# A linear attention block with a gated feed-forward layer: one call moved in the vector engine's program

## The chip, the cores and the metric

The kernel runs on one core of a Trainium2 chip. The core's engines are TensorE (PE; its weight loads are listed apart, as PEld), VectorE (DVE), ScalarE (ACT), GpSimd (POOL) and SyncE (SP), which here only issues DMAs. The metric is the device time of one execution in microseconds (us), the median of three runs. An engine takes its own instructions strictly in the order in which they are written, and the engines meet at semaphores.

## The reference

Sixteen batches of 512 tokens with 256 channels pass through one block of linear attention and one gated feed-forward layer, with a layer norm after each:

```python
qkv = relu(x @ qkv_weight.T)                      # 32 heads of 8 channels: q, k, v
vk   = einsum('bnhe,bnhd->bhed', [v, 1], k)       # per batch and head, 9 x 8
vk_q = einsum('bhed,bnhd->bnhe', vk, q)           # 8 numerators and 1 denominator
att  = vk_q[..., :8] / (vk_q[..., 8:] + 1e-15)
x1   = layernorm(x + att @ proj_weight.T + proj_bias)
h    = silu(x1 @ wg.T) * (x1 @ wu.T)              # wg, wu, wd: integers / 127; hidden 768
out  = layernorm(x1 + h @ wd.T)
```

All of it is float32. The kernel gets that precision from TensorE by splitting each operand into a high part (rounded to fp32r) and a low part (the value minus the high part), so each product is two or three matmuls.

## The kernel before

The 16 batches go through a software pipeline. Step i, for i from 2 to 14, does the feed-forward layer of batch i-1 up to its hidden layer (`ffn_half`), then projection, first layer norm and the turning of batch i, the q, k, v of batch i+1, the down projection of batch i-1, and the attention of batch i+1 (`attention_half`). Steps 2 and 14 are written out, steps 3 to 13 are a hardware loop; the first batches and the last have code of their own. Every engine has its own order, written out by hand; nothing is scheduled by a program.

One step on TensorE is, in order: six gate and up blocks (`gate_up`, j = 0 to 5, eight 128x512 matmuls each), the projection (24 small matmuls), k and v (24), q (12), `vk` (64 tiny ones, L946), the first quarter of the down projection, `num` (64 tiny matmuls, L963, which make numerators and denominators of batch i+1 in the four banks of `abcd_ps`), and three more quarters of the down projection. Then the next step begins with gate block 0, which reads `x1T_hi` and `x1T_lo`.

What the names around the change are:

- `x1T` is the first layer norm's output with channels on the partitions. VectorE transposes it in blocks of 32 (`x1_blocks`, into `wu_raw`), two DMAs out to DRAM and two back in (`wd_raw`, named for the weights that it held before) turn the rest. ScalarE rounds it to `x1T_hi` (L346), VectorE subtracts that (`x1T_lo_spread`, L515): two instructions of 128x512, each with two inputs in SBUF, the engines' common memory.
- `rden_of` waits for `num` (semaphore `num_mm`), then adds the epsilon to the denominators, PSUM to SBUF (`den`, L545, semaphore `den_ok`), and takes the reciprocal (`rden`, L549).
- `att_of` multiplies the numerators in PSUM by `rden` (L567, four instructions). `r2_add` adds the down projection and `x1` (L639, twice). `att_blocks` transposes `att` in blocks (L720, twice).
- GpSimd adds the bias to the next input, `xb` (L296): both inputs in SBUF, 128x1024. It starts when `den_ok` says that `den` of this step is made. GpSimd also makes the inverse deviations, `rstd` (L280).
- `h_of` (L522) makes one of the six blocks of `h` from `up_ps` and `silu`, `h_lo_of` (L515) makes its low part from two inputs in SBUF. `stats_2` (L591) stands between h block 0 and h block 1.

On TensorE the weight load for x1T of gate block 0 waits for both `x1T_lo`; that of gate block 1 waits for the first `r2_add`, since the block overwrites a down bank. From block 2 on, the gate part waits for `silu` of block j-2 and the up part for `h` of block j-2, which free the PSUM banks of that block. ScalarE's order in a step is silu 0, h_hi 0, silu 1, h_hi 1, silu 2, h_hi 2, silu 3, the two `attT_hi`, h_hi 3, silu 4, silu 5, h_hi 4 and 5; a silu stands behind the h_hi before it.

Of the kernel before, what the change touches and what calls it, by code (L numbers as in the profile page):

```python
# [38 lines left out]
def build(nc, x, xT, q_w, kv_w, proj_w, bias, gate_w, up_w, down_w, shape_consts, out):  # L39
    ctx = ExitStack()  # L40
    with ctx:
# [467 lines left out]
        def _(dve):  # L509
# [4 lines left out]
            def minus_hi(lo, raw, hi):  # L514
                return nc.vector.tensor_tensor(lo, raw, f32(hi), ALU.subtract)  # L515
# [10 lines left out]
            def h_lo_of(b, *blocks):  # L526
                for j in blocks:
                    dve.wait_ge(h_hi_ok[j], b + 1)
                    minus_hi(h_lo[:, j, :], h[:, j, :], h_hi[:, j, :]).then_inc(h_lo_ok[j], 1)

            def xT_lo_of(b):
                dve.wait_ge(xT_hi_ok, b)
                minus_hi(xT_lo[:], xT_raw[:], xT_hi[:]).then_inc(xT_lo_ok, 1)

            def vk_of(b, bank=CC):

                dve.wait_ge(vk_mm, b + 1)
                vkv = bank[:, 0:KC * VW].rearrange("p (k n) -> p k n", k=KC)
                nc.vector.tensor_tensor(vk[:], vkv.unsqueeze(2).to_broadcast([P, KC, 2, NW]),
                                        own[:].unsqueeze(1).to_broadcast([P, KC, 2, NW]), ALU.mult).then_inc(vk_ok, 1)  # L540

            def rden_of(b):

                dve.wait_ge(num_mm, b + 1)
                nc.vector.tensor_scalar(  # L545
                    den[:].rearrange("p m (t g u) -> p m (t g) u", t=NT, g=2),
                    num_ps[:, :, :, :, GC:NW].rearrange("p m t g u -> p m (t g) u"), DEN_EPS, None, ALU.add).then_inc(den_ok, 1)
                dve.wait_ge(den_ok, b + 1)
                nc.vector.reciprocal(rden[:], den[:]).then_inc(rden_ok, 1)  # L549

            def att_of(b, turned=False):

                dve.wait_ge(rden_ok, b + 1)
                if turned:

                    for t in range(NT):
                        for m in range(2 * KC):
                            last = nc.vector.tensor_tensor(
                                att[:, t, m // 2 * P:(m // 2 + 1) * P].rearrange("p (u e j) -> p j u e", j=NG, e=HD)
                                [:, m % 2 * 2:m % 2 * 2 + 2],  # L560
                                num_ps[:, m, t, :, 0:GC].rearrange("p j (u e) -> p j u e", e=HD),
                                rden[:, m, t * 2 * GH:(t + 1) * 2 * GH].rearrange("p (j u) -> p j u", j=2)
                                .unsqueeze(3).to_broadcast([P, 2, GH, HD]), ALU.mult)
                    last.then_inc(att_ok, 1)
                    return
                for t in range(NT):
                    last = nc.vector.tensor_tensor(  # L567
                        att[:, t, :].rearrange("p (m g u e) -> p m g u e", g=2, u=GH, e=HD),
                        num_ps[:, :, t, :, 0:GC].rearrange("p m g (u e) -> p m g u e", e=HD),
                        rden[:, :, t * 2 * GH:(t + 1) * 2 * GH].rearrange("p m (g u) -> p m g u", u=GH)  # L570
                        .unsqueeze(4).to_broadcast([P, 2 * KC, 2, GH, HD]),
                        ALU.mult)
                last.then_inc(att_ok, 1)
# [38 lines left out]
            def r1_of(b):  # L612

                if not isinstance(b, int) or b > 1:
                    dve.wait_ge(x1_copied, 16 * (b - 1))
                else:
                    dve.wait_ge(x1_pair[1], 1)
                dve.wait_ge(xb_ok, b + 1)
                for n in range(2):
                    r1_pair(b, n)  # L620
                    stats(st1, r1, n, st1_ok if n else None)
# [14 lines left out]
            def r2_add(b, n, x1_of_b):  # L636

                dve.wait_ge(down_mm[n], b + 1)
                nc.vector.scalar_tensor_tensor(  # L639
                    out=pair(r2, n), in0=down_ps[n], scalar=WSCALE, in1=pair(x1_of_b, n), op0=ALU.mult, op1=ALU.add).then_inc(r2_ok[n], 1)  # L640
# [23 lines left out]
            def x1_of(b, dst):  # L664
                dve.wait_ge(rstd1_ok, b)
                normed(dst, r1, mv1, rstd1, x1_ok)

            def out_of(b):

                if not isinstance(b, int) or b > 0:  # L670
                    dve.wait_ge(stored, 16 * b)
                dve.wait_ge(rstd2_ok, b + 1)
                normed(out_sb, r2, mv2, rstd2, out_ok)
# [49 lines left out]
            def x1_blocks(b):  # L723
                dve.wait_ge(x1_ok, b)
                blocks_turned(x1_sq, r1, x1_sq_ok)

            def att_blocks(b):
                dve.wait_ge(att_ok, b + 1)
                blocks_turned(att_sq, att, att_sq_ok)

            def T_lo_spread(b, T_raw, T_hi, T_hi_ok, T_lo, T_lo_ok):
                for k in range(KC):
                    dve.wait_ge(T_hi_ok[k], b + 1)
                    minus_hi(by_token(T_lo, k), spread(T_raw, k), by_token(T_hi, k)).then_inc(T_lo_ok[k], 1)
# [4 lines left out]
            def x1T_lo_spread(b):  # L739
                T_lo_spread(b, x1T_raw, x1T_hi, x1T_hi_ok, x1T_lo, x1T_lo_ok)  # L740
# [24 lines left out]
            def variance_1(i):  # L765
                dve.wait_ge(st1_ok, i)
                nc.vector.tensor_copy(st1_seen[:], st1[:, NT - 1, 0:1])
                aggregated(st1, mv1, mv1_ok)
                variance(i - 1, mv1, mv1_ok, ve1, ve1_ok)
# [29 lines left out]
            def attention_half(i):  # L799
                r1_of(i)  # L800
                variance_1(i)
                h_lo_of(i - 1, 4)
                x1_of(i, r1)
                x1_blocks(i)
                h_lo_of(i - 1, 5)
                out_of(i - 2)
                vk_of(i + 1)
                if not isinstance(i, int) or i + 2 < NB:
                    xT_lo_of(i + 2)
                x1T_lo_spread(i)  # L810
                rden_of(i + 1)
                att_of(i + 1)
                for n in range(2):
                    r2_add(i - 1, n, x1)
                att_blocks(i + 1)
# [3 lines left out]
            first_turn()  # L819
            ffn_half(2)  # L820
            attention_half(2)

            with dve.Fori(3, NB - 2) as i:
                ffn_half(i)
                attention_half(i)

            ffn_half(NB - 2)
            attention_half(NB - 2)

            i = NB - 1  # L830
# [40 lines left out]
            i = NB  # L871
# [339 lines left out]
```

## Time and profile before

| | |
|---|---|
| runs | 501.08, 502.88, 500.78 us |
| median | 501.08 us |
| profiled execution, its own time | 501.08 us |
| its span | 498.9 us |
| TensorE busy | 490.4 us (98%), mean granted clock 0.997 |
| VectorE busy | 421.8 us (85%) |
| ScalarE busy | 228.7 us (46%) |
| GpSimd busy | 87.8 us (18%) |

The span goes from the first instruction's start to the last one's end; 2.2 us of the run's time lie outside it. TensorE's matmuls are pipelined, so their busy shares overlap, and "98%" says only that there is hardly a moment without one. A line of a timeline gives the start, the length, the engine, the source line, the operation, its output and inputs with shapes, and in brackets the idle time before it with what ended it. Where several instructions of one group follow each other they are merged into one line with their count.

### The profile page before, as it was taken

The numbers are of one execution on the slowest core, as the hardware profiler recorded it, in microseconds if no ns is written. First come the engines' busy times: TensorE is split into PE (matmuls) and PEld (weight loads), VectorE is DVE, ScalarE is ACT, GpSimd is POOL, SyncE is SP. The second block draws the span as 40 slices with busy tenths as digits, with TensorE's granted clock in tenths as the row PEclk, the third lists the DMA queues.
The fourth block names the chain that finished last, engine by engine and source line by source line (L and its number), as shares of the span: only waits on it lengthen the run. The fifth ranks groups of instructions, "written<-read, shape, count | busy, mean of one in ns | idle before, by whom it ended". The sixth has DMA issues, their size and how long they took to land.

```text
span 498.9 us, 11667 instructions
## 1 busy us (share of the span) xinstructions
PE 490.4 (98%) x4588; PEld 422.3 (85%) x4588; DVE 421.8 (85%) x986; ACT 228.7 (46%) x384; POOL 87.8 (18%) x69
## 2 busy tenths in 40 slices
PE   8999999999999999999999999999999999999995
PEld 5788888988888888888988888888888988888785
DVE  5778998788989888798888989889798888978996
ACT  4665354353643535444353543535444353533343
POOL 1220211112113111121121113111131122113102
PEclk9999999999999999999999999999999999999998
DMA  8312252343624235351343524335252343424102
GB/s 318 153 38 85 85 177 79 129 168 126 210 84 157 96 133 203 111 193 75 131 164 126 209 84 140 115 126 210 100 191 88 131 164 126 168 82 147 68 9 79
DMA packets 48306, 65.79 MB, mean 132 GB/s; under 512 B 2977, under 2 KB 32417, under 8 KB 48289
## 3 DMA queue, kind: packets, MB, share of 16 engines
q1 hardware_dynamic: 48144, 65.29, 37.3%
q8 instruction: 12, 0.20, 0.2%
q10 hardware_dynamic: 144, 0.26, 0.2%
q14 instruction: 6, 0.04, 0.0%
HBM read 35.14 MB, written 23.07 MB: 117 GB/s over the span
## 4 chain that ended last, share of the span: by engine, by line
PE 87%; DVE 6%; issue 3%; DMA 2%; POOL 1%; ACT 0%; POOLq 0%; DVEq 0%
PE abcd_ps L918 30%; PE gate_ps L918 26%; PE up_ps L918 25%; PE abcd_ps L963 3%; PE abcd_ps L946 2%; DVE h L522 1%; POOL rstd L280 1%; DMA wq_raw<-w_q 1%; DVE st L591 1%; DVE x1T_lo L515 1%; DMA wd_raw<-x_way 1%; DVE h_lo L515 0%; DVE wg_raw L720 0%; DMA x_way<-wu_raw 0%; ACT x1T_hi L346 0%
## 5 line engine op out<-in xcount | busy, mean ns | idle before, releaser
L351 ACT ACTIVATE silu<-gate_ps 128x512 f32<-128x512 f32 x95 | 55.7, 588 | 79.7 <-PE gate_ps L918 79.7
L280 POOL TENSOR_TENSOR rstd<-ve,minus_half 128x4 f32<-128x4 f32 (+2 forms) x37 | 44.9, 1213 | 253.4 <-DVE ve L603 253.4
L346 ACT ACTIVATE h_hi<-h 128x512 fp32r<-128x512 f32 (+1 forms) x97 | 60.7, 626 | 58.2 <-DVE h L522 57.1
L918 PE MATMUL gate_ps<-x1T_hi,wg_hi 128*128 128x512 f32 x192 | 75.3, 392 | 0.8 <-DVE x1T_lo L515 0.6
L918 PE MATMUL up_ps<-x1T_hi,wu_hi 128*128 128x512 f32 x192 | 74.9, 390 | 0.2 <-DVE h L522 0.2
L918 PE MATMUL gate_ps<-x1T_lo,wg_hi 128*128 128x512 f32 x192 | 75.0, 391 | 0.0
L918 PE MATMUL up_ps<-x1T_lo,wu_hi 128*128 128x512 f32 x192 | 74.7, 389 | 0.0
L522 DVE SCALAR_TENSOR_TENSOR h<-up_ps,silu 128x512 f32<-128x512 f32 x95 | 65.0, 685 | 11.4 <-ACT silu L351 9.4
L515 DVE TENSOR_TENSOR h_lo<-h,h_hi 128x512 fp32r<-128x512 f32 (+1 forms) x97 | 65.1, 672 | 0.2
L296 POOL TENSOR_TENSOR xb<-x_raw,bias_sb 128x1024 f32<-128x1024 f32 x16 | 38.5, 2403 | 144.4 <-DVE den L545 143.4
L343 ACT ACTIVATE kv<-abcd_ps 128x512 f32<-128x512 f32 x55 | 32.9, 601 | 64.9 <-PE abcd_ps L918 64.9
L918 PE MATMUL gate_ps<-wd_hi,h_hi 128*128 128x256 f32 x174 | 46.1, 300 | 0.6 <-issue 0.5
L591 DVE BATCH_NORM_STATS2 st<-r 128x6 f32<-128x256 f32 x124 | 45.0, 413 | 1.1
L918 PEld LDWEIGHTS up_ps<-x1T_hi,wu_hi 128*128 128x128 f32 x192 | 36.0, 188 | 8.4 <-DVE h L522 0.6
L918 PE MATMUL abcd_ps<-wkv_hi,xT_lo 128*128 128x512 f32 x110 | 43.1, 392 | 0.0
L918 PEld LDWEIGHTS gate_ps<-x1T_hi,wg_hi 128*128 128x128 f32 x192 | 36.1, 188 | 8.2 <-DVE x1T_lo L515 1.3
L918 PE MATMUL abcd_ps<-wkv_hi,xT_hi 128*128 128x512 f32 x110 | 43.0, 391 | 0.0
L918 PE MATMUL gate_ps<-wd_hi,h_lo 128*128 128x256 f32 x174 | 42.9, 282 | 0.0
L918 PE MATMUL up_ps<-wd_hi,h_hi 128*128 128x256 f32 x174 | 42.5, 283 | 0.0
L918 PE MATMUL up_ps<-wd_hi,h_lo 128*128 128x256 f32 x174 | 42.4, 283 | 0.0
L918 PEld LDWEIGHTS up_ps<-x1T_lo,wu_hi 128*128 128x128 f32 x192 | 36.0, 188 | 7.5
L918 PE MATMUL abcd_ps<-wkv_lo,xT_hi 128*128 128x512 f32 x110 | 42.3, 389 | 0.0
(169 smaller groups left out, 1023.7 us busy)
## 6 DMA issues: line engine op xcount, KB each, us to landing
x_raw<-x_tok SPq DMA_DIRECT2D x16, 512.0 KB, 6.2
out<-out_sb SPq DMA_DIRECT2D x15, 512.0 KB, 2.6
xT_raw<-x_chan SPq DMA_DIRECT2D x14, 512.0 KB, 6.6
x_way<-wu_raw SPq DMA_DIRECT2D x28, 256.0 KB, 2.1
wd_raw<-x_way SPq DMA_DIRECT2D x28, 256.0 KB, 2.9
att_way<-wg_raw SPq DMA_DIRECT2D x28, 256.0 KB, 2.1
wkv_raw<-att_way SPq DMA_DIRECT2D x28, 256.0 KB, 3.0
x<-r SPq DMA_DIRECT2D x14, 512.0 KB, 4.5
```

The lines of the kernel that those rows point to most:

```text
L280: nc.gpsimd.tensor_tensor(rs[:, tiles], ve[:, tiles], minus_half[:, tiles], ALU.pow).then_inc(rs_ok, 1)
L296: nc.gpsimd.tensor_tensor(xb[:].rearrange("p (t c) -> p t c", t=NT), x_raw[:].rearrange("p (t c) -> p t c", t=NT), bias_sb[:].unsqueeze(1) ...
L343: nc.scalar.activation(dst, src, ACT.Relu).then_inc(ok, 1)
L346: nc.scalar.activation(dst, src, ACT.Copy).then_inc(ok, 1)
L351: nc.scalar.activation(silu[:, j % 2, :], gate_ps[bank_of(b, j)][:], ACT.Silu, scale=WSCALE).then_inc(silu_ok[j], 1)
L515: return nc.vector.tensor_tensor(lo, raw, f32(hi), ALU.subtract)
L522: nc.vector.scalar_tensor_tensor(out=h[:, j, :], in0=up_ps[bank_of(b, j)][:], scalar=WSCALE, in1=silu[:, j % 2, :], op0=ALU.mult, op1=ALU. ...
L591: last = nc.vector.bn_stats(st[:, t, :], r[:, t, :])
L918: last = mm(dst, lhsT, rhs, start=start and n == 0, stop=stop and n == len(pairs) - 1)
L946: vk_mm_last = mm(bank[g * GC:(g + 1) * GC, k * VW:(k + 1) * VW], kv[:, t, n, 0:GC], kv[:, t, KC * NGC + n, :], start=t == 0, stop=t == NT ...
L963: last = mm(num_ps[o:o + HP, 2 * k + half, t, :, :].rearrange("p g n -> p (g n)"), q[rows, k, t * P + o:t * P + o + HP], vk[rows, k, :, :] ...
```

## The change

In `attention_half` of VectorE's program, `rden_of(i + 1)` is written ahead of `x1T_lo_spread(i)` instead of behind it. Nothing is added or taken away, and the other engines' programs are the same.

```diff
                 vk_of(i + 1)
                 if not isinstance(i, int) or i + 2 < NB:
                     xT_lo_of(i + 2)
+                rden_of(i + 1)
                 x1T_lo_spread(i)
-                rden_of(i + 1)
                 att_of(i + 1)
                 for n in range(2):
                     r2_add(i - 1, n, x1)
```

`attention_half` stands in three places, so the order changes there, for 13 steps (2, 3 to 13, and 14). On VectorE, in the loop of steps 3 to 13:

```order
 L539 TENSOR_TENSOR vk<-abcd_ps,own 128x144
 L515 TENSOR_TENSOR xT_lo<-xT_raw,xT_hi 128x1024
-L515 TENSOR_TENSOR x1T_lo<-wd_raw,x1T_hi 128x512 x2
-L545 TENSOR_SCALAR den<-abcd_ps 128x128
-L549 RECIPROCAL rden<-den 128x128
+L545 TENSOR_SCALAR den<-abcd_ps 128x128
+L549 RECIPROCAL rden<-den 128x128
+L515 TENSOR_TENSOR x1T_lo<-wd_raw,x1T_hi 128x512 x2
 L567 TENSOR_TENSOR att<-abcd_ps,rden 128x256 x4
 L639 SCALAR_TENSOR_TENSOR r<-gate_ps,x 128x512
```

The two `x1T_lo` have moved behind `den` and `rden`, and directly ahead of `att`. On VectorE in step 14, where no `xT_lo` is left to make:

```order
 L652 TENSOR_SCALAR out_sb<-r,mv,rstd 128x256 x4
 L539 TENSOR_TENSOR vk<-abcd_ps,own 128x144
-L515 TENSOR_TENSOR x1T_lo<-wd_raw,x1T_hi 128x512 x2
-L545 TENSOR_SCALAR den<-abcd_ps 128x128
-L549 RECIPROCAL rden<-den 128x128
+L545 TENSOR_SCALAR den<-abcd_ps 128x128
+L549 RECIPROCAL rden<-den 128x128
+L515 TENSOR_TENSOR x1T_lo<-wd_raw,x1T_hi 128x512 x2
 L567 TENSOR_TENSOR att<-abcd_ps,rden 128x256 x4
 L639 SCALAR_TENSOR_TENSOR r<-gate_ps,x 128x512
```

The same pieces have changed places, with `vk` directly ahead of them. On GpSimd, whose loop over the steps is the same before and now (`xb` of a step, then `rstd` of the second and of the first layer norm):

```order
L293 REGISTER_ALU [waits den_ok]
L296 TENSOR_TENSOR xb<-x_raw,bias_sb 128x1024 [waits r1_ok1,x_in]
L279 REGISTER_ALU
L280 TENSOR_TENSOR rstd<-ve,minus_half 128x4 [waits ve2_ok]
L280 TENSOR_TENSOR rstd<-ve,minus_half 128x4 [waits ve1_ok]
```

No row has moved here, but the wait for `den_ok` now points to an instruction that stands ahead of the two `x1T_lo`, not behind them.

## Rows read from the trace of the kernel before

**Rows 1.** The page's busy times: us, share of the span, instructions.
```profile
PE 490.4 (98%) x4588; PEld 422.3 (85%) x4588; DVE 421.8 (85%) x986; ACT 228.7 (46%) x384; POOL 87.8 (18%) x69
```
**Rows 2.** The waits: us in total, times, longest.
```profile
POOL xb L296 <- DVE den L545: 143.4, 15, 11.0
...
PEld gate_ps L918 <- DVE x1T_lo L515: 1.3, 3, 0.8
```
**Rows 3.** One stretch: its length, busy us of PE, PEld, DVE, ACT, POOL, clock.
```profile
237.00:267.00 30.00, 30.00 (x312) 26.15 (x300) 25.70 (x59) 13.71 (x24) 5.18 (x3) 1.00 0.40 140
```
**Rows 4.** VectorE's timeline in one loop step: start, length, instruction, idle before.
```profile
240.82 0.69 DVE L515 TENSOR_TENSOR x1T_lo<-wd_raw,x1T_hi 128x512 fp32r<-128x512 f32 x1 [0.52 <-ACT x1T_hi L346]
241.43 0.28 DVE L545 TENSOR_SCALAR den<-abcd_ps 128x128 f32<-128x128 f32 x1
241.74 0.95 DVE L549 RECIPROCAL rden<-den 128x128 f32<-128x128 f32 x1
242.73 1.42 DVE L567 TENSOR_TENSOR att<-abcd_ps,rden 128x256 f32<-128x256 f32 x4
...
248.54 0.69 DVE L522 SCALAR_TENSOR_TENSOR h<-up_ps,silu 128x512 f32<-128x512 f32 x1
...
252.29 0.69 DVE L522 SCALAR_TENSOR_TENSOR h<-up_ps,silu 128x512 f32<-128x512 f32 x1 [0.59 <-ACT silu L351]
```
**Rows 5.** The same step's timeline: `num` on TensorE, `xb` on GpSimd.
```profile
238.82 1.23 PE L963 MATMUL abcd_ps<-vk,qT 64*64 64x72 f32 x64
...
241.93 2.42 POOL L296 TENSOR_TENSOR xb<-x_raw,bias_sb 128x1024 f32<-128x1024 f32 x1 [9.87 <-DVE den L545]
```
**Rows 6.** The same step's weight loads: gate 0, up 3, up 5.
```profile
244.27 0.19 PEld L918 LDWEIGHTS gate_ps<-x1T_hi,wg_hi 128*128 128x128 f32 x1
...
250.31 0.19 PEld L918 LDWEIGHTS up_ps<-x1T_hi,wu_hi 128*128 128x128 f32 x1
...
253.94 0.19 PEld L918 LDWEIGHTS up_ps<-x1T_hi,wu_hi 128*128 128x128 f32 x1
```
**Rows 7.** Timeline around step 2: `num`, `att`, h block 1, up 3's load.
```profile
88.89 1.23 PE L963 MATMUL abcd_ps<-vk,qT 64*64 64x72 f32 x64
...
93.93 1.42 DVE L567 TENSOR_TENSOR att<-abcd_ps,rden 128x256 f32<-128x256 f32 x4
...
99.67 0.69 DVE L522 SCALAR_TENSOR_TENSOR h<-up_ps,silu 128x512 f32<-128x512 f32 x1
...
100.42 0.19 PEld L918 LDWEIGHTS up_ps<-x1T_hi,wu_hi 128*128 128x128 f32 x1
```
**Rows 8.** Timeline: where GpSimd and VectorE run at once, in three places.
```profile
11.56 1.76 DVE L515 TENSOR_TENSOR wg_lo<-wg_raw,wg_hi 128x1536 fp32r<-128x1536 int32 x1
11.67 1.69 POOL L307 COPY own<-consts 64x8 f32<-64x8 f32 x1
...
13.72 0.19 POOL L307 COPY own<-consts 64x8 f32<-64x8 f32 x1
...
52.34 1.02 POOL L280 TENSOR_TENSOR rstd<-ve,minus_half 128x4 f32<-128x4 f32 x1 [14.66 <-DVE ve L603]
52.78 0.68 DVE L515 TENSOR_TENSOR h_lo<-h,h_hi 128x512 fp32r<-128x512 f32 x1
...
249.63 0.68 DVE L515 TENSOR_TENSOR h_lo<-h,h_hi 128x512 fp32r<-128x512 f32 x1
249.80 1.39 POOL L280 TENSOR_TENSOR rstd<-ve,minus_half 128x4 f32<-128x4 f32 x1 [5.45 <-DVE ve L603]
```
**Rows 9.** ScalarE's timeline in the same step as Rows 4: h_hi 2, silu 3.
```profile
251.14 0.63 ACT L346 ACTIVATE h_hi<-h 128x512 fp32r<-128x512 f32 x1 [0.76 <-DVE h L522]
251.67 0.58 ACT L351 ACTIVATE silu<-gate_ps 128x512 f32<-128x512 f32 x1
```
**Rows 10.** Timeline behind step 14: VectorE's `out_sb`, TensorE's load for up 4.
```profile
461.01 0.73 DVE L652 TENSOR_SCALAR out_sb<-r,mv,rstd 128x256 f32<-128x256 f32 x2 [0.98 <-POOL rstd L280]
...
462.40 0.19 PEld L918 LDWEIGHTS up_ps<-x1T_hi,wu_hi 128*128 128x128 f32 x1 [0.59 <-DVE h L522]
```

## The prediction, made before the changed kernel ran

> **What bounds the kernel now.** I read four views, in this order. The page's busy times [rows 1] put TensorE at 98% and VectorE at 85%. A share can hide gaps, so next one whole step of the loop by stretches: from 237 to 267 us TensorE is busy for 30.00 of 30.00 us at full clock, VectorE for 25.70 [rows 3]. So TensorE sets the time, one step is 30 us, and nothing that VectorE saves can shorten the loop; VectorE matters only where it makes TensorE wait. The waits, third, show how rarely that is: TensorE's loads wait for `x1T_lo` three times in the run, 1.3 us in all, and GpSimd's `xb` waits for `den` 15 times [rows 2]. Last, the timeline around the moved instructions, for how much cover each hand-over has [rows 4 to 7].
>
> **What the change moves, without anything new in the way.** Take the step of rows 4. `num` ends at 238.82 + 1.23 = 240.05 [rows 5]. Before, VectorE does both `x1T_lo` first (the second is held up by `x1T_hi` and starts at 240.82), then `den` at 241.43, `rden` at 241.74, `att` at 242.73 [rows 4]. So `den` goes to `rden` in 0.31 us, `rden` to the next in 0.99, and an `x1T_lo` to the next in 0.61. After the change `den` waits for `num` itself. A semaphore takes about 0.06 us to act: h block 1 of step 2 ends at 99.67 + 0.69 = 100.36 and the load that wants it is at 100.42 [rows 7]. So `den` starts at 240.11, `rden` at 240.42, VectorE is free at 241.41, the `x1T_lo` start at 241.41 and 242.02, and `att` at 242.63, which is 0.10 earlier than 242.73. The later `x1T_lo` ends at 242.02 + 0.69 = 242.71, and gate block 0 wants it at 244.27 [rows 6]: cover 1.56 us. By this alone the time does not move: the 1.3 us by which `rden` comes earlier are given to `x1T_lo`, and TensorE hides both.
>
> **What else the moved `den` releases.** `xb` on GpSimd starts 0.50 us behind `den` (241.43 to 241.93) and lasts 2.42 [rows 4, 5]. It now starts at 240.61 and ends at 243.03. Before, only `rden`, `att` and `r2_add` ran beside it, none of which has two inputs in SBUF. Now both `x1T_lo`, which have two, want to start inside it, at 241.41. No row of the trace has this pair with `xb` first, so its price is bounded from both sides.
>
> The rows that bear on it: a GpSimd copy of 64x8 takes 1.69 us when it starts 0.11 us after VectorE's `wg_lo`, an instruction with two SBUF inputs, and ends at 13.36, just behind its end at 13.32. The same copy takes 0.19 us with VectorE idle. So it began in effect at 13.17, 0.15 before the end of `wg_lo`'s record. `rstd` beside `h_lo`, again two SBUF inputs and started first, takes 1.39 us, where it takes 1.02 beside `h` [rows 8]; 0.37 more puts its effective start at 250.17, 0.14 before `h_lo` ends at 250.31. Both say that GpSimd stands still until VectorE's reads are over. That is a wait for a shared reader, and a shared reader held by GpSimd should stop VectorE too.
>
> Against it: `h_lo` at 52.78 starts inside `rstd` (52.34 to 53.36) and takes its usual 0.68 [rows 8]. But `rstd` reads four numbers for each partition and then computes, so its reads may be over by then, while `xb` reads 1024 numbers twice and can hardly have finished 0.8 us after its start. I lean to the held reader.
>
> The Trainium skill ("SBUF — State Buffer", section "Who interferes with whom") states this as a rule: a VectorE instruction with two SBUF inputs contends with a GpSimd instruction that reads SBUF, whichever starts first keeps the shared port for the whole instruction, and the other fully blocks. The copy and the `rstd` beside `h_lo` agree with it; the `h_lo` inside `rstd` does not fit its "whole instruction". Taken literally it would release `x1T_lo` only at the end of `xb`, not 0.14 us before, and without it this prediction would be "no change".
>
> **The price if `xb` holds `x1T_lo` up.** The first `x1T_lo` starts between 243.03 - 0.14 = 242.89 and 243.03; I take 242.96. The second starts at 243.57 and ends at 244.26, so TensorE sees it at 244.32, 0.05 behind its load at 244.27 [rows 6]: almost nothing. But `att` starts at 243.57 + 0.61 = 244.18 instead of 242.73, and everything behind it on VectorE (two `r2_add`, two transposes, h block 0, four statistics, h block 1) was back to back, so h block 1 is late by the same 1.45 us. It starts at 248.54 + 1.45 = 249.99, ends at 250.68 and is seen at 250.74; up block 3 wants it at 250.31 [rows 4, 6]: 0.43 late.
>
> The point from which this decides can be read in step 2, where `x1T` came late by itself. There `num` ends at 88.89 + 1.23 = 90.12 and `att` starts 3.81 us later, against 242.73 - 240.05 = 2.68 in rows 4 and 5: 1.13 late. h block 1 reached TensorE at 100.42, and the load went at once [rows 7]; its usual place is 90.12 + (250.31 - 240.05) = 100.38. So 1.13 us is just what TensorE hides, and 1.45 is past it.
>
> Behind h block 1 a chain takes over: h block 1, h_hi 1, silu 2, h block 2, h_hi 2, silu 3, h block 3, since ScalarE does each silu behind the h_hi before it. One link is 0.69 + 0.03 for h, 0.53 from h_hi to silu, 0.58 + 0.04 for silu [rows 4, 9]: 1.87 us. TensorE's blocks take (253.94 - 250.31) / 2 = 1.81 [rows 6]. So each of two blocks loses 0.06 more: h block 3 starts at 249.99 + 2 x 1.87 = 253.73, is seen at 254.48, and up block 5 wants it at 253.94: 0.54 late. These delays of one step are not added, since each is counted against the undisturbed TensorE; the largest counts. A block is eight matmuls, 1.81 / 8 = 0.23 us each, and a weight load can go that far ahead of its matmul, so 0.54 costs TensorE between 0.31 and 0.54; I take 0.43. For the bounds: `xb` releasing earlier and the lead absorbing all gives 0.2, `attT_lo` for the projection slipping too gives 0.6. After the projection VectorE has idle time again, so nothing is carried into the next step.
>
> Steps 2 to 13 pay this: 12 x 0.43 = 5.2 us (2.4 to 7.2). Step 14 differs. Behind it VectorE waits for `rstd` and makes half of `out_sb` ahead of h block 2, and the load for up block 4 already waits 0.59 us for that h [rows 10]. No cover is left there, so up to the whole 1.45 reaches TensorE; I take 1.3 (0.9 to 1.5). Sum: 5.2 + 1.3 = 6.5 us, bounds 3.3 and 8.7. The profiled execution took 501.08 us, which is also the median of the runs, so the sum stands against 501.08: **507.6 us**, own range 504.4 to 509.8.
>
> What else changes queue costs nothing. SP gets `att_blocks` 1.45 us later and so starts the turning of `att`, the copy of r1 and the two loads later; they have until the projection and the next step. `xb` itself is done 1.3 us earlier and is wanted only at the next projection.
>
> **The rivals.** (1) *No hold-up*: GpSimd's reads give way or share, `x1T_lo` runs at 0.69 each. Then the first part's working holds: 1.56 us of cover, `att` 0.10 earlier, step 2's late `att` back in line, and 501.1 us, not slower. For it speak the `h_lo` inside `rstd` and that TensorE waits for nothing in the loop; against it the two GpSimd rows that stood still. It decides if `att` is late by less than 1.13 us. (2) *Sharing by turns*: both `x1T_lo` at half speed until `xb` ends. The first takes 1.3 us instead of 0.61, the second starts at 242.7 and is half done at 243.03, so `att` starts near 243.5, 0.8 late, under 1.13: 501.1 again. (3) *The delay is carried over*: VectorE, pushed behind in the feed-forward half, also comes late to the layer norm and the next `num`, and a step loses more than 0.6. At 1.0 a step: 12 + 1.5, or 514.6. Against it is the 4.30 us in a step in which VectorE is idle [rows 3]. (4) *Faster*: earlier `rden` removes a TensorE wait. TensorE has none in the loop to remove; even the 1.3 us of rows 2 are mostly in code that is not changed.
>
> **How the numbers follow.** Hold-up as priced 0.60, of which about 0.04 ends within 0.5%; rival 1 0.26; rival 2 0.07; rival 3 0.05; faster 0.02. About 0.5% (2.5 us) is what a measurement of this kernel can tell from no change. Slower: 0.56 + 0.05 and 0.03 for a partial hold-up with a higher price than rival 2 has, 0.64. Same: 0.26 + 0.04 + 0.04 = 0.34. Faster 0.02. The time is the likeliest case's, 507.6. The range must reach the unchanged cases, which hold a third: 500.6 to 509.8.
>
> **What the profile after would show.** Right: `xb` 1.3 us closer behind `num`; the first `x1T_lo` starting (or ending, if its record begins before the hold) with `xb`'s end instead of 1.3 us behind `den`; `att` about 4.1 us behind `num`'s end, not 2.7; TensorE's loads of up blocks 3 to 5 waiting for h in each of 12 steps, 0.3 to 0.6 in sum, steps of 30.4 us; and a wait above 1.5 us behind step 14. Wrong: two `x1T_lo` of 0.69 starting 1.3 us behind `den` inside `xb`. Then `att` stands at 2.6 and TensorE stays gapless. If `x1T_lo` is held and TensorE still does not wait, the cover behind `att` was read wrong.

## The result and the profile after

| | before | after |
|---|---|---|
| median of 11 runs | 502.61 us | 506.31 us |
| lowest | 500.69 us | 505.73 us |
| ratio after to before, 95% interval | | 1.0095 [1.0065, 1.0124] |
| profiled execution: its time, its span | 501.08, 498.9 us | 507.97, 506.0 us |

The change costs about 0.95%. On 501.08 us, the time before that the prediction was set against, the ratio is 4.8 us (3.3 to 6.2), or 505.8 us against the 507.6 forecast. The profiled execution of the changed kernel lies 1.7 us above its median; 1.9 us of its span were lost in step 1, which the change doesn't touch (below).

The page's busy times of the changed kernel (answering to [rows 1]: us, share of the span, instructions), then one whole step by stretches (answering to [rows 3]: length, then busy us of PE, PEld, DVE, ACT, POOL):

```profile
PE 494.3 (98%) x4588; PEld 416.2 (82%) x4588; DVE 438.1 (87%) x986; ACT 227.5 (45%) x384; POOL 87.8 (17%) x69
```

```profile
239.00:269.30 30.30, 30.30 (x286) 25.61 (x285) 26.95 (x60) 13.56 (x24) 5.16 (x3) 1.00 0.39 138
```

TensorE still shows no gap, at full clock, and yet the step is longer: its short waits are listed only at its weight loads. VectorE makes the same 986 instructions and is "busy" for 16.3 us more, a sign of something that the busy column can't show, an engine that stands inside an instruction. The step's length is plain from `num`. The timeline of the changed kernel in two steps running, then of the kernel before in the step behind that of [rows 5]:

```profile
242.40 1.23 PE L963 MATMUL abcd_ps<-vk,qT 64*64 64x72 f32 x64
...
272.70 1.23 PE L963 MATMUL abcd_ps<-vk,qT 64*64 64x72 f32 x64
```

```profile
268.78 1.23 PE L963 MATMUL abcd_ps<-vk,qT 64*64 64x72 f32 x64
```

That is 30.30 us a step against 268.78 - 238.82 = 29.96 before. Where it goes shows in the timeline around the moved instructions (answering to [rows 4, 5]), VectorE and GpSimd of the changed kernel:

```profile
243.69 0.29 DVE L545 TENSOR_SCALAR den<-abcd_ps 128x128 f32<-128x128 f32 x1 [0.72 <-PE abcd_ps L963]
244.02 0.95 DVE L549 RECIPROCAL rden<-den 128x128 f32<-128x128 f32 x1
244.89 2.27 DVE L515 TENSOR_TENSOR x1T_lo<-wd_raw,x1T_hi 128x512 fp32r<-128x512 f32 x1
...
247.08 0.68 DVE L515 TENSOR_TENSOR x1T_lo<-wd_raw,x1T_hi 128x512 fp32r<-128x512 f32 x1
247.68 1.40 DVE L567 TENSOR_TENSOR att<-abcd_ps,rden 128x256 f32<-128x256 f32 x4
```

```profile
244.21 2.40 POOL L296 TENSOR_TENSOR xb<-x_raw,bias_sb 128x1024 f32<-128x1024 f32 x1 [8.15 <-DVE den L545]
```

The first `x1T_lo` takes 2.27 us for work of 0.69. Its record begins where it was due, and it ends 0.55 us behind `xb`. The second starts at 247.08; one `x1T_lo` follows another by 0.61, so the first began in effect at 246.47, 0.14 before `xb` ends at 246.61. `att` starts 4.05 us behind `num`'s end (243.63), against 2.68 before: 1.37 us late. TensorE pays for it at its weight loads (answering to [rows 6]):

```profile
249.74 0.19 PEld L918 LDWEIGHTS gate_ps<-x1T_hi,wg_hi 128*128 128x128 f32 x1 [0.19 <-DVE r L639]
...
254.15 0.19 PEld L918 LDWEIGHTS up_ps<-x1T_hi,wu_hi 128*128 128x128 f32 x1 [0.23 <-DVE h L522]
...
256.03 0.19 PEld L918 LDWEIGHTS up_ps<-x1T_hi,wu_hi 128*128 128x128 f32 x1 [0.16 <-DVE h L522]
...
257.90 0.19 PEld L918 LDWEIGHTS up_ps<-x1T_hi,wu_hi 128*128 128x128 f32 x1 [0.17 <-DVE h L522]
```

These are gate block 1, which waits for `r2_add`, and up blocks 3, 4 and 5, which wait for h. In the waits of the whole run (us in total, times, longest), these lines of the changed kernel are new or have grown. Before, `den` had 1.3 us in 2 waits, the up blocks for h 0.6 in one, the gate for `x1T_lo` 1.3 in 3, and the last two lines were not there:

```profile
DVE den L545 <- PE abcd_ps L963: 12.3, 15, 2.5
...
PEld up_ps L918 <- DVE h L522: 8.2, 36, 1.7
...
PEld gate_ps L918 <- DVE x1T_lo L515: 3.2, 3, 2.1
...
PEld gate_ps L918 <- DVE r L639: 2.3, 12, 0.2
PEld abcd_ps L918 <- DVE attT_lo L515: 2.2, 12, 0.2
```

The hold itself is in none of them. It is seen only where `x1T_lo` is listed by its durations (min, median, max in ns):

```profile
L515 DVE TENSOR_TENSOR x1T_lo<-wd_raw,x1T_hi x28: 677/693/2279, 63.4 to 459.0; 128x512 fp32r<-128x512 f32 x28
```

Behind step 14 the load for up block 4 (answering to [rows 10]) waits 1.68 us, not 0.59:

```profile
469.51 0.19 PEld L918 LDWEIGHTS up_ps<-x1T_hi,wu_hi 128*128 128x128 f32 x1 [1.68 <-DVE h L522]
```

Steps 2 to 13 together are read from `num` of step 2 to `num` of step 14, in the changed kernel and then in the kernel before (whose `num` of step 2 is in [rows 7]):

```profile
90.88 1.23 PE L963 MATMUL abcd_ps<-vk,qT 64*64 64x72 f32 x64
...
454.50 1.23 PE L963 MATMUL abcd_ps<-vk,qT 64*64 64x72 f32 x64
```

```profile
448.54 1.23 PE L963 MATMUL abcd_ps<-vk,qT 64*64 64x72 f32 x64
```

That is 363.62 against 359.65 us, 4.0 more. It is a little less than 12 x 0.34, since step 2 of the kernel before was itself longer than the others, 30.09 us. With 1.68 - 0.59 = 1.1 us behind step 14 the profile accounts for 5.1 us, within the interval of the ratio.

The 2.1 us wait for `x1T_lo` in the list above is at 66.37 us, in step 1. There SP's two issues for `x_way` took 2.10 us together in this execution and 0.91 in the profiled one of the kernel before, `x1T` came late, and TensorE stood. The kernels of the experiments had this long wait in some profiles (2.32 us in that of e1_xb_behind) and not in others (0.33 in that of e7_step14_only); in e2 and e3 the two issues took 0.91 us and the data landed late. I don't count it to the change.

The times follow it. From `num` of step 1 to `num` of step 2 the kernel before takes 30.26 us, and the four experiments without the long wait (e5, e7, e9, c2) 30.1 to 30.5. The changed kernel takes 32.14 and e6 32.15. And e1, e2, e3, e4 and e8 take 33.8 to 34.4, because there the granted clock falls behind the wait to 0.50, the lower of its two levels (1.2 GHz), for some 3 us. Two stretches of e1, laid out as in [rows 3], with the clock behind the five engines:

```profile
66.00:68.00 2.00, 2.00 (x6) 1.63 (x7) 2.00 (x4) 0.07 (x1) 1.82 (x1) 0.69 0.00 0
68.00:70.00 2.00, 2.00 (x6) 1.52 (x6) 1.06 (x3) 0.53 (x1) 0.56 (x1) 0.50 0.69 260
```

The profiled executions of e1, e3 and e8 lie 3.4, 3.6 and 4.1 us above their medians, that of e2, which has four of its six runs near it, 0.3, that of the changed kernel 1.7, and none without the long wait more than 0.1. So a median also tells how many of its runs had the wait. The lowest runs, 500.69 and 505.73 us, differ by 5.0, close to the 5.1 of the profile.

### The profile page after: what moved, and what is told of

Its sections match the earlier page's. It is cut to its first block, busy times and chain, and to the rows that moved or that the text cites. A ratio compares the mean times of both kernels' runs of the same rounds, so it can differ in the third digit from the quotient of the medians.

```text
span 506.0 us, 11667 instructions
## 1 busy us (share of the span) xinstructions
PE 494.3 (98%) x4588; PEld 416.2 (82%) x4588; DVE 438.1 (87%) x986; ACT 227.5 (45%) x384; POOL 87.8 (17%) x69
## 4 chain that ended last, share of the span: by engine, by line
PE 86%; DVE 9%; DMA 2%; ACT 1%; issue 1%; POOL 0%; POOLq 0%; DVEq 0%
PE abcd_ps L918 31%; PE gate_ps L918 25%; PE up_ps L918 24%; PE abcd_ps L963 3%; PE abcd_ps L946 2%; DVE h L522 1%; DVE x1T_lo L515 1%; DVE h_lo L515 1%; DMA wq_raw<-w_q 1%; DMA wd_raw<-x_way 1%; DVE st L591 1%; DMA x_way<-wu_raw 1%; DVE r L608 0%; DVE att L558 0%; DVE attT_lo L515 0%
## 5 line engine op out<-in xcount | busy, mean ns | idle before, releaser
L351 ACT ACTIVATE silu<-gate_ps 128x512 f32<-128x512 f32 x95 | 54.5, 587 | 70.8 <-PE gate_ps L918 70.8
L918 PE MATMUL up_ps<-x1T_hi,wu_hi 128*128 128x512 f32 x192 | 76.4, 398 | 1.2 <-DVE h L522 1.2
L918 PEld LDWEIGHTS gate_ps<-x1T_lo,wg_hi 128*128 128x128 f32 x192 | 36.1, 188 | 7.0 <-issue 0.2
```

The lines of the kernel that those rows point to most:

```text
L351: nc.scalar.activation(silu[:, j % 2, :], gate_ps[bank_of(b, j)][:], ACT.Silu, scale=WSCALE).then_inc(silu_ok[j], 1)
L918: last = mm(dst, lhsT, rhs, start=start and n == 0, stop=stop and n == len(pairs) - 1)
```

## The experiments

The theory, HOLD: `xb` on GpSimd keeps the reads that `x1T_lo`, with two inputs in SBUF, needs, because the moved `den` starts `xb` ahead of `x1T_lo`. The rival, ORDER: the new order on VectorE costs the time by itself, whatever GpSimd does.

**The order without the overlap.** The changed kernel, with one wait of GpSimd pointed elsewhere:

```diff
-                pool.wait_ge(den_ok, i + 1)
+                pool.wait_ge(x1T_lo_ok[KC - 1], i)
                 xb_of(i)
...
-            pool.wait_ge(den_ok, NB)
+            pool.wait_ge(x1T_lo_ok[KC - 1], NB - 1)
```

> The changed kernel's order on VectorE, but GpSimd's xb of steps 2 to 14 waits for the second x1T_lo instead of den, so the two never overlap. Theory HOLD (xb holds the reads that x1T_lo needs): x1T_lo runs at 0.69 us each from 1.3 us behind den, att starts 2.6 us behind num's end instead of 4.05, TensorE is gapless in the loop again (step 29.96 us), and the time is that of the kernel before: ratio 0.997 to 1.002. Theory ORDER (the later x1T_lo and the VectorE order by themselves cost the time): the ratio stays at 1.007 to 1.010, with steps of 30.3 us.

Measured: 500.62 us, ratio to the kernel before 0.9968 [0.9944, 0.9992]. VectorE's timeline in a step where `num` ends at 241.94 + 1.23 = 243.17, and GpSimd's `xb`:

```profile
243.23 0.29 DVE L545 TENSOR_SCALAR den<-abcd_ps 128x128 f32<-128x128 f32 x1 [0.72 <-PE abcd_ps L963]
...
244.43 1.22 DVE L515 TENSOR_TENSOR x1T_lo<-wd_raw,x1T_hi 128x512 fp32r<-128x512 f32 x2
245.57 1.41 DVE L567 TENSOR_TENSOR att<-abcd_ps,rden 128x256 f32<-128x256 f32 x4
```

```profile
245.88 2.40 POOL L296 TENSOR_TENSOR xb<-x_raw,bias_sb 128x1024 f32<-128x1024 f32 x1 [10.70 <-DVE x1T_lo L515]
```

Both `x1T_lo` take 1.22 us together, `att` stands 2.40 us behind `num`, and the whole cost is gone with VectorE's new order in place. ORDER falls.

**The overlap without the order.** The kernel before, with `xb` released by `num`:

```diff
-                pool.wait_ge(den_ok, i + 1)
+                pool.wait_ge(num_mm, i + 1)
                 xb_of(i)
...
-            pool.wait_ge(den_ok, NB)
+            pool.wait_ge(num_mm, NB)
```

> The kernel before with its own VectorE order, but xb is released by num on TensorE instead of by den, about 1.3 us earlier. Theory HOLD: xb starts about 0.2 us behind num's end, where the second x1T_lo wants to start 0.8 us behind it, so that x1T_lo is held until xb ends at +2.6, den starts at +3.2, att at +4.5 (before: +2.7): worse than the changed kernel, steps of 30.5 to 30.7 us, ratio 1.015 to 1.02. Theory ORDER: VectorE's order is the old one, so the ratio is 0.998 to 1.002.

Measured: 519.25 us, ratio 1.0316 [1.0275, 1.0356]. Slower as HOLD says, and by more than I had priced. Of the 18.4 us between the two spans 13.5 lie in steps 2 to 13, 1.9 behind `num` of step 14, and 3.0 ahead of step 2, where this profile has the long wait of step 1. VectorE's and GpSimd's timeline, with `num` ending at 246.98 + 1.23 = 248.21:

```profile
248.40 3.50 DVE L515 TENSOR_TENSOR x1T_lo<-wd_raw,x1T_hi 128x512 fp32r<-128x512 f32 x2 [0.84 <-ACT x1T_hi L346]
251.83 0.28 DVE L545 TENSOR_SCALAR den<-abcd_ps 128x128 f32<-128x128 f32 x1
...
253.13 1.42 DVE L567 TENSOR_TENSOR att<-abcd_ps,rden 128x256 f32<-128x256 f32 x4
```

```profile
248.47 2.89 POOL L296 TENSOR_TENSOR xb<-x_raw,bias_sb 128x1024 f32<-128x1024 f32 x1 [7.81 <-PE abcd_ps L963]
```

Here the first `x1T_lo` starts 0.07 us ahead of `xb`, so `xb` stands first (2.89 us, not 2.40), and then the second `x1T_lo` stands until `xb` is through, at 251.36. `att` comes 4.92 us behind `num`, 2.24 late, and the next `num` starts at 278.15: a step of 31.17 us (the others take 30.85 to 31.29). I had added only 0.5 to 0.7 us a step, having taken `att` at 4.5 and the loss behind the threshold too low; it is one for one.

**Reads or the whole port.** The changed kernel, where from batch 2 on GpSimd writes only, but for one column (the bias and the residual input are left out of the result; the branch that keeps batches 0 and 1 as they were isn't shown):

```diff
-                nc.gpsimd.tensor_tensor(
-                    xb[:].rearrange("p (t c) -> p t c", t=NT), ...
+                nc.gpsimd.tensor_tensor(xb[:, 0:1], x_raw[:, 0:1], bias_sb[:, 0:1], ALU.add)
+                nc.gpsimd.memset(qT_first[:], 1.0)
+                nc.gpsimd.memset(x1_last[:], 1.0)
+                nc.gpsimd.memset(xb[:, 1:], 1.0).then_inc(xb_ok, 1)
```

> The changed kernel, where from batch 2 on GpSimd's xb is replaced by a 1-column add and three fills of 1024 columns (xb itself and two unused buffers), so GpSimd works for 2 to 3 us at the same place but only writes; the bias and the residual input are left out of the result. Theory HOLD by the reads: x1T_lo takes 0.69 us each beside the fills, att stands 2.6 us behind num's end, about 501 us. Theory HOLD by the whole shared port, reads and writes: x1T_lo waits for the fills as it waited for xb, steps of 30.2 us or more, 505 us or more. ORDER: 505 to 508 us whatever GpSimd does.

Measured in a single run: 504.97 us. It has a wait of 2.78 us for `x1T` in step 1 like the one above, with the clock's fall behind it: 34.43 us from `num` of step 1 to `num` of step 2, where the kernel before has 30.26. Without these 4.2 us it would be about 501 (an estimate), as the hold of the reads alone has it. One run is little, so the verdict is read in the step, VectorE's and GpSimd's timeline (`num` ends at 242.87 + 1.23 = 244.10):

```profile
245.36 1.22 DVE L521 TENSOR_TENSOR x1T_lo<-wd_raw,x1T_hi 128x512 fp32r<-128x512 f32 x2
246.50 1.41 DVE L573 TENSOR_TENSOR att<-abcd_ps,rden 128x256 f32<-128x256 f32 x4
```

```profile
244.80 0.96 POOL L302 MEMSET qT_first<- 128x1024 f32 x1
245.69 0.95 POOL L303 MEMSET x_last<- 128x1024 f32 x1
```

Both `x1T_lo` run at full speed inside two fills, `att` stands 2.40 us behind `num`, and steps 3 to 13 take 29.96 us each. The forecast for the step held: the hold is on the reads, not on the writes.

**How long one hold lasts.** Three kernels change only the length or the pieces of `xb` in the changed kernel. First, four instructions of 256 columns (the lines added; they stand in place of the one addition):

```diff
+                for t in range(NT):
+                    last = nc.gpsimd.tensor_tensor(xb[:, t * C:(t + 1) * C], x_raw[:, t * C:(t + 1) * C], bias_sb[:], ALU.add)
+                last.then_inc(xb_ok, 1)
```

> The changed kernel, where xb is four additions of 128x256 (about 0.6 us each) instead of one of 128x1024 (2.4). If the hold lasts one GpSimd instruction: the first x1T_lo waits for the piece under way only, at most 0.6 us, and the second at most for one more, so att stands 3.0 to 3.7 us behind num's end (after: 4.05), less late than the 1.13 us that TensorE hides, steps of 29.96 us, ratio 0.998 to 1.003. If GpSimd keeps the reads over instructions that follow each other: att at 4.05 or later as in the changed kernel, ratio 1.007 or more. ORDER, already refuted, would give 1.007 to 1.010.

Measured: 502.3 us, ratio 1.0002 [0.9972, 1.0031]. Timelines of VectorE, of the second `x1T_lo` alone and of GpSimd (`num` ends at 242.61 + 1.23 = 243.84):

```profile
245.11 1.77 DVE L515 TENSOR_TENSOR x1T_lo<-wd_raw,x1T_hi 128x512 fp32r<-128x512 f32 x2
```

```profile
245.65 1.23 DVE L515 TENSOR_TENSOR x1T_lo<-wd_raw,x1T_hi 128x512 fp32r<-128x512 f32 x1
246.80 0.41 DVE L567 TENSOR_TENSOR att<-abcd_ps,rden 128x256 f32<-128x256 f32 x1
```

```profile
244.43 3.74 POOL L297 TENSOR_TENSOR xb<-x_raw,bias_sb 128x256 f32<-128x256 f32 x4 [8.57 <-DVE den L545]
```

The second `x1T_lo` stands for one piece, 0.55 us; `att` is 2.96 us behind `num`, 0.28 late, and TensorE hides it: the steps take 29.96 us. The pieces take 3.74 us, since they stand for `x1T_lo` in turn. In step 14 both `x1T_lo` are held, `att` is 3.48 us behind `num`, and the load behind it waits 1.32 us instead of 0.59, so 0.7 us of the cost stays; the ratio doesn't resolve it.

Second, half of the columns from batch 2 on (the residual's other half is left out; here and in e9 below the branch for batches 0 and 1 isn't shown):

```diff
-                    xb[:].rearrange("p (t c) -> p t c", t=NT), x_raw[:].rearrange("p (t c) -> p t c", t=NT),
-                    bias_sb[:].unsqueeze(1).to_broadcast([P, NT, C]), ALU.add).then_inc(xb_ok, 1)
+                    xb[:, 0:2 * C].rearrange("p (t c) -> p t c", t=NT // 2), x_raw[:, 0:2 * C].rearrange("p (t c) -> p t c", t=NT // 2),
+                    bias_sb[:].unsqueeze(1).to_broadcast([P, NT // 2, C]), ALU.add).then_inc(xb_ok, 1)
```

> The changed kernel, where from step 2 on xb adds only the first 512 of 1024 columns (the rest keeps old values, so half of the residual is left out), about 1.2 us instead of 2.4. HOLD: x1T_lo is held 0.3 us instead of 1.5, att 2.9 us behind num's end, TensorE gapless in the loop, ratio 0.998 to 1.003. A hold that doesn't depend on the length of xb would leave 1.007 or more.

Measured: 502.04 us, ratio 0.9995 [0.9963, 1.0028], with `xb` of 1.30 us, both `x1T_lo` in 1.77, `att` 2.96 us behind `num` and steps of 29.96 us.

Third, the same sum twice, first into a buffer that nobody reads:

```diff
+                if not isinstance(b, int) or b >= 2:
+                    nc.gpsimd.tensor_tensor(
+                        qT_first[:].rearrange("p k n -> p (k n)").rearrange("p (t c) -> p t c", t=NT), ...
```

> The changed kernel, where GpSimd makes the same sum first into an unused buffer and then into xb (4.8 us instead of 2.4). Three outcomes, all with HOLD. GpSimd keeps the reads through both: x1T_lo starts 2.4 us later, att 6.5 us behind num's end, steps of 32.7 us, about 535 us. VectorE gets one x1T_lo in between and the second waits for the second sum: att at 7 us, steps of 33.3 us, about 545 us. VectorE gets both in between: as the changed kernel, 505 to 508 us.

Measured: 547.87 us, ratio 1.0932 [1.0876, 1.0988], which is the second outcome. Timelines of GpSimd and of the second `x1T_lo`:

```profile
258.97 2.41 POOL L297 TENSOR_TENSOR qT_first<-x_raw,bias_sb 128x1024 f32<-128x1024 f32 x1 [8.14 <-DVE den L549]
261.34 2.81 POOL L300 TENSOR_TENSOR xb<-x_raw,bias_sb 128x1024 f32<-128x1024 f32 x1
```

```profile
261.85 2.85 DVE L519 TENSOR_TENSOR x1T_lo<-wd_raw,x1T_hi 128x512 fp32r<-128x512 f32 x1
```

The two engines take turns by whole instructions: first sum, first `x1T_lo` (for which the second sum stands 0.4 us), second sum, second `x1T_lo`. No instruction is slowed by sharing within it, which settles rival 2 of the prediction.

The time, close to the 545 us expected, is less of a hit than it looks. `att` stands 6.24 us behind `num`, not 7. Four of the twelve steps from `num` to `num` run at full clock and take 32.48 us. In the other eight the granted clock falls to 0.50 for some 3 us behind TensorE's wait of 2.07 us for the second `x1T_lo` (0.95 in the mean of the step), and they take 33.7. The clock falls once more behind step 14. At full clock throughout, the profiled execution of 546.66 us would have been about 535, an estimate from nine times 1.25 us less: as the first outcome has it. The timeline tells the two apart, the time does not.

**Where it begins to cost.** The changed kernel with `xb` of 896 columns from batch 2 on (the last 128 are left out, and the bias is taken from its first 128 columns):

```diff
-                    xb[:].rearrange("p (t c) -> p t c", t=NT), x_raw[:].rearrange("p (t c) -> p t c", t=NT),
-                    bias_sb[:].unsqueeze(1).to_broadcast([P, NT, C]), ALU.add).then_inc(xb_ok, 1)
+                    xb[:, 0:7 * P].rearrange("p (t c) -> p t c", t=7), x_raw[:, 0:7 * P].rearrange("p (t c) -> p t c", t=7),
+                    bias_sb[:, 0:P].unsqueeze(1).to_broadcast([P, 7, P]), ALU.add).then_inc(xb_ok, 1)
```

> The changed kernel, where xb from step 2 on adds 896 of 1024 columns (the rest keeps old values), 2.1 us instead of 2.4. It tests the point from which the hold costs, 1.13 us read from step 2 of the kernel before. att should stand 3.75 us behind num's end, 1.07 late instead of 1.37. If 1.13 is right: TensorE waits for no h in steps 2 to 13, steps of 29.96 to 30.0 us, only step 14 costs 0.8 us, ratio 1.000 to 1.003. If the loss is instead in proportion to the hold, a step costs 0.27 us and the ratio is 1.006 to 1.008.

Measured: 503.11 us, ratio 1.0049 [1.0019, 1.0079]. The expectation missed both ways: `num` starts at 119.21 and 149.26, steps of 30.05 us, in a step where `att` starts 3.78 us behind `num`, 1.10 late. Neither of the two expectations holds: it is not 0, and not the 0.27 of proportion, but 0.09. With the others the points lie on one line:

| | `att` behind `num` | late against 2.68 | step | lost in a step |
|---|---|---|---|---|
| e3_xb_quarters, e5_xb_half | 2.96 | 0.28 | 29.96 | 0.00 |
| e9_xb_896 | 3.78 | 1.10 | 30.05 | 0.09 |
| before, step 2 | 3.81 | 1.13 | 30.09 | 0.13 |
| after | 4.05 | 1.37 | 30.30 | 0.34 |
| e7_step14_only, step 2 | 4.08 | 1.40 | 30.34 | 0.38 |
| e2_xb_at_num | 4.92 | 2.24 | 31.17 | 1.21 |

The loss is the lateness less 1.0 us, or the distance of `att` from `num` less 3.7. (The 2.68 is one step's; in steps 3 to 13 of the kernel before it goes from 2.39 to 2.87, with `x1T_hi` sooner or later, and each of them takes 29.96.) Two rows have VectorE's old order: step 2 of the kernel before, and step 2 of e7 below, where `x1T` came late by itself. They lose what the others lose, so it is the lateness that costs and not what makes it.

Step 2 of the kernel before: `num` starts at 88.89 and 118.98 there, a step of 30.09. I had read from [rows 7] that 1.13 is hidden in full, because the load went at once and no wait was listed; the step's length tells that it isn't. A timeline leaves out waits of up to 0.15 us, and TensorE's loads for up 3, 4 and 5 have gaps of 0.06 to 0.10 us there.

**The two parts of the change.** Step 14 alone (`attention_half` has the new order only where `i == NB - 2`), and steps 2 to 13 alone:

```diff
+                if isinstance(i, int) and i == NB - 2:
+                    rden_of(i + 1)
                 x1T_lo_spread(i)
-                rden_of(i + 1)
+                if not (isinstance(i, int) and i == NB - 2):
+                    rden_of(i + 1)
```

> The change in step 14 alone; steps 2 to 13 keep the order of the kernel before. HOLD: TensorE's wait for h ahead of up block 4 behind step 14 grows from 0.59 to 1.7 us, nothing else changes: 1.1 us slower, ratio 1.002 to 1.003. With the 12 other steps at 0.34 us each (4.1 us) that makes the whole change. ORDER: the same, if the price of step 14 is of that size; this run sizes, it doesn't tell the two apart.

The other kernel has the same lines with the two conditions exchanged:

> The change in steps 2 to 13 alone; step 14 keeps the order of the kernel before. Steps of 30.30 us instead of 29.96, 12 of them, and TensorE's wait behind step 14 stays at 0.6 us: 4.1 us slower, ratio 1.007 to 1.0085; together with the 1.1 us of step 14 alone the whole change. If the loss of a step weren't additive (VectorE late in one step, so the next one is later), step 14 in the old order would still lose time and the ratio be that of the whole change, 1.0095.

Measured: step 14 alone 502.27 us, ratio 1.0029 [1.0001, 1.0056]; steps 2 to 13 alone 505.2 us, ratio 1.0079 [1.0053, 1.0106]. The parts make 1.0108 together, the whole change 1.0095, the same within the intervals. The load behind step 14, in the first and in the second kernel:

```profile
463.89 0.19 PEld L921 LDWEIGHTS up_ps<-x1T_hi,wu_hi 128*128 128x128 f32 x1 [1.69 <-DVE h L522]
```

```profile
470.68 0.19 PEld L921 LDWEIGHTS up_ps<-x1T_hi,wu_hi 128*128 128x128 f32 x1 [0.91 <-DVE h L522]
```

0.91 us, where I expected 0.6: of what steps 2 to 13 lose, at most 0.3 us is carried behind the last of them. `att` stands 3.06 us behind `num` in step 14 there, against 2.70 in the kernel before.

**A version to keep.** e1 with two more moves on VectorE, at the places where the profile of the kernel before shows TensorE waiting:

```diff
                 x1_of(1, r1)
+                x1_blocks(1)
                 h_of(0, 5)
                 h_lo_of(0, 4)
-                x1_blocks(1)
...
+            h_of(i - 1, 2)
             dve.wait_ge(stored, 16 * (i - 2))
             dve.wait_ge(rstd2_ok, i - 1)
             normed(out_sb, r2, mv2, rstd2, out_ok, range(2))
-            h_of(i - 1, 2)
```

> e1 (the changed order, xb behind x1T_lo) and two more moves on VectorE. In step 1 the block transposes of x1 stand ahead of h block 5 and h_lo 4 instead of behind them, so the turning by DMA starts 1.2 us earlier and TensorE's wait for x1T at the start of step 2 (0.24 us in the kernel before, 2.1 us in the changed one) goes: 0.2 to 1.2 us less. Behind step 14 h block 2 stands ahead of half of out_sb, so that the wait of 0.59 us for it goes: 0.4 us less. Against e1 0.6 to 1.6 us less, 499 to 500 us, ratio to before 0.993 to 0.998. If the stall in step 1 just moves to the wait for the down projection's h block 5, 500.2 us.

Measured: 500.73 us, ratio 0.9976 [0.9953, 0.9999], no better than e1 at 500.62 and 0.9968 [0.9944, 0.9992]; the 499 to 500 us expected were missed. The wait for h block 2 is gone, but the projection's load then waits 0.68 us for `attT_lo`: the stall moved. In step 1 the wait for `x1T` is down to 0.08 us, but a load waits 0.35 us for h block 5, as the end of the expectation has it. What the first move seems to buy is less scatter: in this profile SP's two issues for `wd_raw` took 3.01 us and TensorE hardly waited, and the highest of the 12 runs is 501.97 us, where 11 of the 29 of the kernel before beside it are above 502.9. That the move does it was not tried alone. Both versions beat the changed kernel by over 1% and the kernel before by about 0.3%, at the edge of what the runs can tell. Of e1's 0.3% (1.6 us) only the late `x1T` of step 2, which no longer holds up `rden`, has a place: 0.13 us in the profile of the kernel before, 0.38 in that of e7. Part of the rest can be how many runs had the wait of step 1; it stays open.

## Why the prediction was right, step by step

- *TensorE bounds, and the order alone costs nothing.* Right: e1 has the order and not the cost. Rival 1, at 0.26, had the same time for another reason, reads of GpSimd that give way, and the held `x1T_lo` rules that out.
- *`den` at 0.06 us behind `num`, `xb` at 0.56, ending at 2.98.* Measured 0.06, 0.58, 2.98.
- *A shared reader held by GpSimd stops VectorE.* Right, and this was the step with the least behind it: [rows 8] show only the other direction, VectorE first, and the forecast itself says that without the Trainium skill's rule it would have been "no change". The release 0.14 us before the end of `xb` was forecast, half counted, and measured as 0.14. Had I taken it whole, `att` would have been 1.38 late; measured 1.37, forecast 1.45. What spoke against it, `h_lo` inside `rstd`, is no contradiction with a hold of the reads alone, as e4 shows reads to be what counts. That `rstd` ends its reads early remains argued.
- *The Trainium skill's rule* ("SBUF — State Buffer", "Who interferes with whom"), two SBUF inputs against a GpSimd instruction that reads SBUF, the first to start keeps it and the other blocks: borne out in both directions and with its exception for GpSimd instructions that only write (e4). Its "whole instruction" is close, but the release came 0.14 us before the end of the record.
- *`x1T_lo` itself reaches gate block 0 just in time.* Right, that load doesn't wait in the loop.
- *0.43 us a step, from h block 3.* The mechanism and its places hold (waits at up 3, 4 and 5: 0.23, 0.16 and 0.17), the size was 0.34. 0.08 of the difference is the release above. The other part of the term, how much of a late load TensorE's lead takes up, came out nearly right by two errors that cancel. `att` is 1.37 late, but h block 1 only 1.29 (9.78 us behind `num` against 8.49), so up 5's load is 257.90 - 243.63 = 14.27 us behind `num`, 0.38 more than before, where the working gives 0.46 for the hold as measured. And of the 0.38 TensorE took up 0.04, not 0.11. The chain of h, h_hi and silu is as forecast: from h block 1 to h block 3 it takes 257.16 - 253.41 = 3.75 us, 2 x 1.87. The 1.02 us that the working has as hidden at up 3 (250.31 less 249.29, when h block 1 was there) is what the table shows; the 1.13 read from step 2, by which the rivals were judged, is too high. I left out the wait of gate block 1 for `r2_add` (0.19), which comes earlier and is contained in the later ones.
- *1.3 us behind step 14.* Measured 1.1. There `xb` starts 0.44 us behind `num`, not 0.58, so the hold is shorter: `att` stands 3.91 us behind `num`, against 2.70 before, 1.21 late, and nearly all of it reaches TensorE, as the forecast said. e7, with the old order up to step 13, has the same 3.91 and a wait of 1.69.
- *Sum 6.5 us.* Measured 4.8 (3.3 to 6.2), by the profile 5.1. Too high in both terms, by 1.2 and 0.2; 0.1 of the first is that step 2 of the kernel before had already lost it.
- *Nothing is carried over (rival 3).* Right but for up to 0.3 us at the last step (e8).

## What to carry to other kernels

A semaphore that an instruction signals moves with the instruction: before moving one, list who waits for it on other engines and what will then run beside what. Where VectorE instructions with two SBUF inputs stand near a GpSimd instruction that reads SBUF, release the latter behind them, from a VectorE instruction that is followed by work on PSUM; here that wait alone was worth 1%. And judge cover by the step's length, not by whether a wait is listed.

## What the runs showed of the hardware that I had not expected

- The hold counts as busy time. VectorE's busy time rose from 421.8 to 438.1 us with the same instructions, `x1T_lo` from 692 to 1414 ns in the mean, and no list of waits has a line for it.
- The two engines alternate by whole instructions even when GpSimd has two queued (e6): VectorE gets in between them, and then stands for the second. Splitting the GpSimd instruction in four therefore cuts the hold in the loop to one piece, 0.55 us, and the cost there to nothing (e3).
- A hold is symmetrical: `xb` takes 2.40 us alone, and 2.89 with an `x1T_lo` just ahead of it (e2).
- Two issues on SP's queue took 0.91 us in one execution and 2.10 in another at the same place of the same code in step 1, and TensorE waited 2.1 us for it. In profiles with such a wait (2.1 to 2.8 us) the granted clock mostly fell to 0.50 behind it, for some 3 us, and the step came out 3.5 to 4.2 us longer than the 30.26 of the kernel before, not 2. In the changed kernel it stayed at 1.00 behind a wait of 2.10, and in e6 it fell behind eight of twelve waits of 2.07. The runs of most kernels scatter by some 4 us, and the clocks fit: of the 29 runs of the kernel before beside e3, the eight at 504.8 to 505.5 us have a mean granted clock of 0.994 or 0.995, all others 0.997 or more. Whether the wait alone makes the scatter was not tried.
